# Graph network on one core: the message written feature-major, the degree spread by a bf16 product, the turning of the aggregate dropped

## The reference

```python
h = maximum(layernorm(x), 0)                          # 3125 nodes x 256
# first network, 50000 edges, src/dst lists
msg_input  = concat([h[src], h[dst], edge_features])
hid        = relu(msg_input @ mW1 + mb1)              # 512 wide
messages   = hid @ mW2 + mb2                          # 256 wide
aggregated = segment_sum(messages, src)
u          = relu(concat([h, aggregated]) @ uW1 + ub1)
x          = x + h + u @ uW2 + ub2
h = maximum(layernorm(x), 0)
# second network: three layers of segment_sum(norm * (h @ W)[src], dst) + b, gelu between them
x = x + layers(h)
```

## Time and profile before

| | us |
|---|---|
| median of 3 runs | 2052.21 |
| lowest, highest | 2049.65, 2060.61 |
| the profiled execution | 2049.62 |
| its span, first to last instruction | 2047.8 |
| mean granted TensorE clock | 0.925 of full speed |
| fused stage within it | 1217.5 to 1528.5 |

### The profile page before, as it was taken

The page is one execution under the profiler, slowest core; times in us unless marked ns, Lnnn a source line. Parts: engine busy times, 40 slices in busy tenths (PEclk is TensorE's granted clock), DMA queues, the critical chain, the costliest instruction groups (busy, mean ns, idle before and its releaser), DMA issues. The chain is left out here.

```text
span 2047.8 us, 34486 instructions
## 1 busy us (share of the span) xinstructions
PE 1817.7 (89%) x8786; PEld 1237.3 (60%) x8786; DVE 1542.7 (75%) x4650; ACT 797.9 (39%) x1975; POOL 1262.3 (62%) x1463
## 2 busy tenths in 40 slices
PE   4577887777399999999999998989979999999999
PEld 2344544444255555555555556666657888788887
DVE  7887787777489999999999988988988345445333
ACT  0122222222155665665665656656664112113000
POOL 2777777777788888888888859999979000000000
PEclk7677777888699999999999999999999999999999
DMA  5111111111276766666766785222236344343333
GB/s 163 39 58 51 52 58 58 58 58 56 69 197 195 198 195 195 198 195 195 196 196 194 194 173 163 69 66 68 72 92 185 93 124 124 93 126 121 109 108 110
DMA packets 181705, 254.12 MB, mean 124 GB/s; under 512 B 29244, under 2 KB 144761, under 8 KB 181514
## 3 DMA queue, kind: packets, MB, share of 16 engines
q0 software_dynamic: 47888, 126.25, 22.6%
q1 hardware_dynamic: 104696, 102.31, 16.4%
q10 hardware_dynamic: 28930, 23.35, 3.5%
HBM read 202.35 MB, written 49.37 MB: 123 GB/s over the span
## 5 line engine op out<-in xcount | busy, mean ns | idle before, releaser
L1009 POOL DMA_INDIRECT brow<-B_rows,rows x440 | 467.8, 1063 | 114.9 <-issue 58.4
L380 POOL DMA_INDIRECT src_list<-ring,ring_row x392 | 385.8, 984 | 156.7 <-issue 117.6
L1959 PE MATMUL pO<-F,y 128*128 128x512 f32 x1728 | 431.5, 404 | 4.7 <-DVE y L1770 3.2
L1959 PEld LDWEIGHTS pO<-F,y 128*128 128x128 f32 x1728 | 326.7, 190 | 79.8 <-DVE y L1770 4.0
L1332 POOL TENSOR_SCALAR src_oh<-iota,src_s 128x128 bf16<-128x128 bf16 x426 | 285.1, 685 | 39.9 <-PE pC L1475 21.8
L1059 PE MATMUL pNode<-hid_whole,oh 128*128 128x512 f32 x440 | 228.7, 601 | 4.9 <-DVE sums L1195 4.5
L1125 ACT ACTIVATE turned<-pC 128x256 fp32r<-128x256 bf16 x220 | 84.7, 385 | 279.9 <-PE pC L1038 279.9
L1348 DVE TENSOR_SCALAR dst_oh<-iota_cw,dst_s 128x458 bf16<-128x458 f16 x568 | 181.7, 366 | 0.0
L1061 PE MATMUL pNode<-hid_upper,oh 128*128 128x512 f32 x220 | 175.3, 797 | 0.0
L1475 PE MATMUL pC<-dst_oh,src_oh 128*128 128x458 bf16 x568 | 157.4, 361 | 16.6 <-SPq L1430 8.3
L824 PE MATMUL pP<-U,upto 128*128 128x182 bf16 x385 | 49.6, 280 | 136.4 <-DVE posf L587 136.4
(11 more groups left out here) (306 smaller groups left out, 3413.1 us busy)
## 6 DMA issues: line engine op xcount, KB each, us to landing
raw<-C_rows SPq DMA_DIRECT2D x54, 768.0 KB, 4.4
C_rows<-c_rows ACTq DMA_DIRECT2D x175, 114.5 KB, 1.7
raw_first<-C_rows SPq DMA_DIRECT2D x18, 768.0 KB, 4.4
rows<-src_list SPq DMA_DIRECT2D x110, 100.0 KB, 2.8
brow<-B_rows,rows POOLq DMA_INDIRECT x440, 3.8
U_parts<-part_u SPq DMA_DIRECT2D x25, 256.0 KB, 2.0
B_rows<-bst SPq DMA_DIRECT2D x25, 256.0 KB, 2.1
src_list<-ring,ring_row POOLq DMA_INDIRECT x392, 2.2
```

The costliest lines, as they stand in the source:

```text
L380: nc.gpsimd.indirect_dma_start(dr.src_list[:, :, :].rearrange("p t w -> (p t) w"), bass.IndirectOffsetOnAxis(ap=ring_row[:, k % RING, t:t ...
L1009: nc.gpsimd.indirect_dma_start(brow[:, t % BR, :], None, dr.B, bass.IndirectOffsetOnAxis(ap=rows_i[:, m % LCS, j, 1:2], axis=0)).then_inc( ...
L1959: last = mm(pO[m % 2][half][:, :], y[:, win, part, half * P:(half + 1) * P], F[:, n % FS, :], start=(win == 0 and part == 0), stop=False)
```

## The change

In `build_and_update` three things are different, and two types follow from them.

**Message with features on the partitions.** The operands of the message product are exchanged: `mw2` is now the stationary one and `sT` the moving one, so `pG` holds 128 features of the first half, then 128 of the second, by 128 nodes. That is the layout that the hidden product wants in `aggT`. The two transposes of PE (L1534), DVE's `agg` step (L1398) and DVE's copy (L1404) are gone.

**Degree spread over the partitions.** With features on the partitions, `mb2` is a column (one number for each partition, `[P, 2]`), and the degree is a row that every partition needs. A product with the column of `pair_w` repeated 128 times as the stationary operand gives that row on all partitions: four bf16 products in every second turn, for two windows, into the upper half of `pG`. `pair_w` and `degT` become bf16 for it. DVE copies the two rows to `degs` (in every second turn) and makes `aggT` with two instructions of 128 x 128.

**Order on DVE.** This work stands at u = 8 of the same turn, behind L1411 and L1413; it no longer waits at u = 4 and u = 7. SP loads `mb2` as two DMAs of one column each, in place of one that repeats the row over all partitions.

```diff
@@ DVE, build_and_update @@
                     if u == 1 and i == 0:
                         dve.wait_ge(gathered, 1)
-                        v.tensor_copy(keep.deg_src[:, :], pX[:, 0:NW]).then_inc(deg_read, 1)
+                        v.tensor_copy(keep.deg_src[:, :], pX[:, 0:NW]).then_inc(keep.own, 1)
+                        link.n += 1
@@
-                    if u == 4 and i < NW:
-                        dve.wait_ge(agg_done, i + 1)
-                        if i >= 1:
-                            dve.wait_ge(at_done, i)
-                        else:
-                            dve.wait_ge(deg_read, 1)
-                            dve.wait_ge(w_in, 16 * 5)
-                        v.scalar_tensor_tensor(out=agg[:, :], in0=mb2[:, :], scalar=keep.deg_src[:, i:i + 1],
-                                               in1=pG[:, 0:D], op0=ALU.mult, op1=ALU.add).then_inc(agg_ready, 1)
-                    if u == 7 and i < NW:
-                        dve.wait_ge(at_done, i + 1)
-                        if i >= 1:
-                            dve.wait_ge(u_done, i)
-                        v.tensor_copy(aggT[:, :], pG[:, D:2 * D]).then_inc(at_ready, 1)
@@ behind L1413 @@
+                    if u == 8 and i < NW:
+                        dve.wait_ge(agg_done, i + 1)
+                        if i >= 1:
+                            dve.wait_ge(u_done, i)
+                        else:
+                            dve.wait_ge(w_in, 16 * 6)
+                        if i % 2 == 0:
+                            some = min(2, NW - i)
+                            link(v.tensor_copy(degs[:, 0:some, :].rearrange("p n k -> p (n k)"), pG[:, D:D + some * P]))
+                        for q in range(2):
+                            v.scalar_tensor_tensor(out=aggT[:, q * P:(q + 1) * P], in0=degs[:, i % 2, :],
+                                                   scalar=mb2[:, q:q + 1], in1=pG[:, q * P:(q + 1) * P],
+                                                   op0=ALU.mult, op1=ALU.add).then_inc(at_ready, 1)
@@ SP @@
-            sp.dma_start(mb2[:, :], io["L0_gnn_mb2"].partition_broadcast(P)).then_inc(w_in, 16)
+            for q in range(2):
+                sp.dma_start(mb2[:, q:q + 1], io["L0_gnn_mb2"][q * P:(q + 1) * P].rearrange("(p o) -> p o", o=1)
+                             ).then_inc(w_in, 16)
@@ PE, message(i, half) @@
                     if i >= 1:
-                        pe.wait_ge(agg_ready, i)
-                        pe.wait_ge(at_ready, i)
+                        pe.wait_ge(at_ready, 2 * i)
                     else:
-                        pe.wait_ge(w_in, 16 * 5)
-                for k in range(2 * half, 2 * half + 2):
-                    last = mm(pG[:, 0:D], sT[:, k * P:(k + 1) * P], mw2[:, k, :], start=(k == 0), stop=(k == 3))
+                        pe.wait_ge(w_in, 16 * 6)
+                    if i % 2 == 0:
+                        for n in range(min(2, NW - i)):
+                            for m in range(KP):
+                                size = min(P, PAIRS - m * P)
+                                mm(pG[:, D + n * P:D + (n + 1) * P], pair_w[0:size, m, i + n:i + n + 1].to_broadcast([size, P]),
+                                   degT[0:size, m, :], start=(m == 0), stop=(m == KP - 1))
+                for k in range(4):
+                    last = mm(pG[:, half * P:(half + 1) * P], mw2[:, k, half * P:(half + 1) * P],
+                              sT[:, k * P:(k + 1) * P], start=(k == 0), stop=(k == 3))
@@ PE, turn loop @@
-                    if u == 7 and i < NW:
-                        pe.wait_ge(agg_ready, i + 1)
-                        for k in range(2):
-                            last = nc.tensor.transpose(pG[:, D + k * P:D + (k + 1) * P], agg[:, k * P:(k + 1) * P],
-                                                       keep.ident[:, :])
-                        last.then_inc(at_done, 1)
```

More of the change, by code:

```diff
@@ L1259, in build_and_update @@
         dst_oh = g.sb("dst_oh", [P, SLOTS, CW], BF16)
-        mb2 = g.sb("mb2", [P, D])
+        mb2 = g.sb("mb2", [P, 2])
+        degs = g.sb("degs", [P, 2, P])
         late_u = g.sb("late_u", [P, 8, 2, D])
         low, mw2, uw1, uw2 = keep.low, keep.mw2, keep.uw1, keep.uw2
-        agg, aggT = low[:, 16, D:2 * D], low[:, 17, D:2 * D]
+        aggT = low[:, 17, D:2 * D]
         sT, uT = keep.spans[:, 0:HID], keep.spans[:, HID:2 * HID]
@@ L1284, in build_and_update @@
         c_out = keep.c_out
-        deg_read = g.sem("deg_read")
         w_in, h_in = keep.w_in, keep.h_in
@@ L1289, in build_and_update @@
         agg_done = g.sem("agg_done")
-        agg_ready = g.sem("agg_ready")
-        at_done = g.sem("at_done")
         at_ready = g.sem("at_ready")
@@ L1492, in hidden @@
                 if m == 0:
-                    pe.wait_ge(at_ready, w + 1)
+                    pe.wait_ge(at_ready, 2 * w + 2)
                     if w >= 1:
@@ L2089, in build @@
                 keep.iota_cw = more.sb("iota_cw", [P, CW], F16)
-                keep.pair_w = more.sb("pair_w", [P, KP, NW])
+                keep.pair_w = more.sb("pair_w", [P, KP, NW], BF16)
                 keep.part_m = more.sb("part_m", [P, KT])
@@ L2101, in build @@
                                             else keep.spread[:, 8, D + q * P:D + (q + 1) * P])
-                keep.degT = keep.low[:, NW - 1, 0:KP * P].rearrange("p (m k) -> p m k", m=KP)
+                keep.degT = keep.low[:, NW - 1, 0:KP * P // 2].bitcast(BF16).rearrange("p (m k) -> p m k", m=KP)
                 keep.chosen = lambda m, n: keep.rounded[:, (4 * m + 2 * n) * HID:][:, 0:HS]
```

## The result

The changed kernel runs in 2045.17 us (median of 19 runs, 2039.33 to 2054.25) against 2053.81 (median of 19, 2048.87 to 2060.61) for the kernel before: ratio **0.9956, 95% interval 0.9943 to 0.997**, so about 9.0 us less. That is 0.44%: the interval is clear of 1, but the gain is smaller than the half per cent that the prediction asked for before it would say faster. The profiled execution took 2042.46 us (span 2039.7) against 2049.62 (2047.8).

The account below looks back on a forecast made before the run. The chain between DVE and PE was taken to bound the kernel, with POOL and ACT next. -10.6 (waits) + 1.5 (start) = -9.1 us gave 2040.5 from the profiled execution, 2043.1 as a median; range 2036 to 2053.

Parts of the forecast that it names:

- The chain and its cure: Hidden product through DVE to update product, 2.36 us; with the relu done after 1.27, PE's wait of 0.83 us a turn goes.
- Two thirds of 15.9: Three timed stretches of the fused stage: 15.9 us above POOL's and ACT's floors, of which 10.6 was taken as gain.
- POOL's 70.5: Middle stretch of 42 buckets: POOL's busy time, 70.5 us, taken as the floor for its 77.8 us.
- ACT's floor of 91.3: Early stretch of 56 buckets: ACT's own pace would need 91.3 us, taken as the floor for its 96.6 us.
- ACT as the next bound: Fused stage: ACT's own sequence takes 1.63 us a bucket, 10.56 us a turn, and becomes a bound after the change.
- POOL beside it: Fused stage: POOL's one-hots need 10.56 us a turn, so POOL becomes a bound together with ACT.
- POOL's pace: POOL's one-hots stay at 0.669 us each; 0.681 throughout beside a full DVE would cost 4 us of the gain.
- PE's work about 0: Message pieces, removed transposes and degree product on PE sum to about 0, from -0.1 to +0.1 us a turn.
- DVE's new instructions: Two 128-column instructions of 0.34 us each, copy 0.21 a turn; sum 0.91 against 0.89 removed, so no change.
- PE's waits behind the `aggT` block: After the relu DVE stays with aggT, so PE waits 0.1 to 0.5 us for the next dst_oh; such waits rise.
- the `aggT` block starves PE: Rival, chance 0.10: a block behind the relu lasting over 2.1 us starves PE; at 2.6 us +14, so 2066.
- The start: Start of the fused stage: issuing and landing two single-column DMAs of mb2 costs +1.5 us, from +0.7 to +4.4.

Follow-up runs that it names:

- e1: Kernel before, only DVE's copy to aggT (L1404) moved from unit 7 to unit 8 behind the relu; ratio to before 0.9912.
- e2: Kernel before, DVE's copy to aggT moved to unit 8 but ahead of the sum and the relu; ratio to before 0.9923.
- e5: Changed kernel, ACT loads the register with the next bucket's end while the present copy runs; ratio to before 0.9899.
- e11: Kernel before, copy to aggT moved to unit 8 behind the relu and ACT's register load made early; 2033.52 us, ratio to before 0.9909.
- e6: Kernel before, only ACT's register load for the next bucket made early; ratio to before 0.9979.
- e9: Changed kernel plus a tiny ACT copy (128 x 1) ahead of each bank copy; one run, 2061.89 us.
- e10: Kernel before plus a tiny ACT copy (128 x 1) ahead of each bank copy; one run, 2058.56 us.
- e4: Changed kernel plus two dummy f32 transposes a turn on PE at unit 7; ratio to before 0.9959.
- e3: Changed kernel, its aggT block put back to unit 7, ahead of the sum and the relu; ratio to before 1.0066.
- e7: Changed kernel, the two mb2 column DMAs issued at the end of the block before, ahead of the loads of U; ratio to before 0.9913.
- e8: Changed kernel with ACT's register load early and the mb2 column loads early; 2037.27 us, ratio to before 0.9909.

## Why the prediction was right, step by step

The forecast was 2043.1 us, from -10.6 + 1.5 = -9.1; measured were 2045.17 us, and -9.0 by the ratio, -8.6 by stage and medians. That the sums agree to half a microsecond is in part luck, since the two terms missed in opposite directions (-11.4 for -10.6, +2.8 for +1.5). Most of the 2.1 us between forecast and measured time is the base: the kernel before came out at 2053.81 us, not at 2052.2.

- **The chain and its cure: right; the price of the wait was misread.** Hidden to update product 1.24 us from 2.36; relu done 1.15 us after the sum's start, 1.19 after the hidden product (1.27 forecast). e1 shows that the order alone is the gain, and e2 that nearly all of it comes with the one-hots moved ahead of what waits. The 0.83 us a turn that I called PE's loss was 19.2/23 from the row of the weight load; PE's own row gives 12.9/23 = 0.56. That wait went as forecast (0.5 us left in all). DVE's remaining wait is 9.5/16 = 0.6 us in the turns that have one, 0.4 a turn over all, where I said 0.3. The turns took (1495.8 - 1232.5)/24 = 10.97 us (L1407 below), inside the 10.8 to 11.0 named.
- **Two thirds of 15.9: right in the sum, wrong in its parts.** Forecast -10.6, measured -11.4 in the three stretches. The middle one reached the floor (70.7 us for POOL's 70.5, 7.0 of 7.3); the early one got 2.2 of 5.3, the late one 2.2 of 3.3. Two thirds was a mean that held for none of them. Why the early one stays 3.2 us above ACT's floor of 91.3 is open: e5, with a faster ACT, got only 1.0 of it, and e11, with the same ACT and the old products, 2.7. The floors are soft by about 1 us as well: e1 and e11 took 69.7 and 69.3 us in the middle stretch, under POOL's 70.5, which came from 70.48/104 = 0.678 us a one-hot there; e11 made them in 69.29/105 = 0.660.
- **ACT as the next bound: right**, shown from both sides (e5 against e6, e9 against e10). In the three stretches of after 145 of 161 copies come 1.60 to 1.66 us apart, where it had been 123. **POOL beside it: half right.** It was close behind, and became the bound only when ACT was relieved (e11).
- **POOL's pace: right.** 0.660 us with a fuller DVE, not 0.681. The rule of the Trainium skill (page "SBUF — State Buffer", section "Who interferes with whom") has held as far as this row shows: POOL's one-hots got no slower while DVE's busy share rose from 90% to 95%.
- **PE's work about 0: right within what can be seen.** The message is now eight pieces in a row:

```profile
1303.93 1.06 PE L1492 MATMUL pG<-sums 128*128 128x128 f32 x8
```

  One alone lasts 0.275 us, so (1.06 - 0.275)/7 = 0.11 each, half of the 0.21 of a 256-column piece, as the row of the hidden product had said. The rule on load and product pairs from the Trainium skill (page "TensorE: Matmul & The Clock Gate", section "Back-to-back issue gap") would have added 0.22 us a turn; the trace has none of it. The degree product, for which I took 0.15 us a turn, costs less: its four bf16 pieces, each with a weight load of its own, start 0.058 us apart, so 0.23 every second turn, 0.12 a turn. Removing the transposes saved some 2.0 us by e4, and e1, which keeps them, is no slower. The new order alone needs none of this.
- **DVE's new instructions: right.** L1409 took 341 ns (0.34 forecast), L1407 411 to 425 for two windows.

```profile
L1409 DVE SCALAR_TENSOR_TENSOR sums<-degs,mb,pG x50: 326/341/349, 1232.9 to 1496.3; 128x128 f32<-128x128 f32 x50
...
L1407 DVE COPY degs<-pG x13: 278/411/425, 1232.5 to 1495.8; 128x256 f32<-128x256 f32 x12, 128x128 f32<-128x128 f32 x1
```

- **PE's waits behind the `aggT` block: right at the place, wrong in total.** In the corner above PE runs out at 1301.64 and waits 0.28 us, within the 0.1 to 0.5 forecast. But I had expected the sum of PE's waits for `dst_oh` to rise from 6.5 us; it fell to 3.2, most likely since the one-hots made in DVE's former idle time remove such waits elsewhere (e1, with one copy behind the relu, has 1.7). My walk also has a slip: its own terms for an even turn give 1.27 + 1.15 + 0.36 = 2.8 us to the next `dst_oh`, not 2.7; the corner shows 2.66 to PE's start. I had looked at the one place where the change could hurt and not at those where it helped. The rival *the `aggT` block starves PE* needed a block of over 2.1 us; it lasts 0.61 to 1.06.
- **The start: the term was too small.** +1.5 forecast; measured +0.6 to the first bank copy, +1.5 in the first seven buckets, +0.6 behind the last stretch: +2.8 before rounding, inside the bounds of 0.7 to 4.4. The issue did as thought, 0.98 us for two in place of 0.35; landing did not: 2.2 to 3.1 us, less than either value I had.

```profile
1217.68 0.98 SPq L1422 DMA_DIRECT2D mb<-in_L_gnn_mb_dram  x2
...
1220.47 1.22 PE L1475 MATMUL pC<-dst_oh,src_oh 128*128 128x458 bf16 x4 [1.57 <-SPq L1430]
...
1223.83 0.63 PE L1489 MATMUL pG<-sums,pair_w 128*128 128x128 bf16 x4
1224.26 2.02 PE L1492 MATMUL pG<-sums 128*128 128x128 f32 x8
```

  The first message starts at 1224.26, so the columns, landed by 1221.3 at the latest, did not hold it up. What I had not priced is the clock. In after, PE ran at 1.2 GHz (0.50) for 3 us longer:

```profile
1222.00:1225.00 3.00, 2.29 (x10) 1.63 (x11) 3.00 (x12) 1.08 (x2) 3.00 (x5) 0.50 0.43 138
1225.00:1228.00 3.00, 3.00 (x15) 2.66 (x14) 1.53 (x6) 0.00 (x0) 1.24 (x2) 0.50 0.53 164
1228.00:1231.00 3.00, 3.00 (x18) 2.09 (x18) 1.71 (x6) 1.66 (x4) 2.16 (x4) 0.97 0.45 127
```

  Before, the same windows had 0.53, 1.00 and 1.00. Over the traces this goes with the late columns, though not with them alone. All five kernels that load the columns at the start of the stage (after, e3, e4, e5, e9) are at 0.50 for 6.8 us and take 14.5 to 15.9 us for the first seven buckets. The two that load them earlier (e7, e8) are at 0.50 for 3.4 us and take 13.9. Of the seven with the old `mb2`, five have 3.4 us at 0.50, e10 has none and e1 has 6.8; they take 13.0 to 13.6 us, but e1 14.5. In e10 PE had waited for SP at the start about as in before (0.91 and 1.12 us, against 0.91 and 1.21), so these waits alone do not decide it. That the late columns bring the longer stretch at half clock is likely by this count and not shown; the cause is open.

## What to carry to other kernels

When two engines wait for each other, look first at the order in which the waiting engine issues what it has: independent work belongs ahead of the wait, and a single instruction that waits for the same event as a more urgent one behind that one. Here the first half was worth 11.8 us in the stretches (e2) and the second 0.8 more. Size the gain by what the *next* engines leave, stretch by stretch, and check it by making the next engine faster and slower: an edit worth 1 us of the stage before and 7 us after (e6, e5) is the clearest sign that a bound has moved. Read a wait from the row of the engine that does the work, not from that of its weight loads. When a rewrite brings a new order with it, try the order alone; here it was all of the gain, and with one register load moved on ACT more than twice that, -21.6 us against -8.6 in the stage (one trace each) and -0.91% against -0.44% by the ratios, of which the order alone has -0.88%.

## What the runs showed of the hardware

- A register load on ACT's queue, behind a copy, a refill and a store, cost about 0.5 us of each bucket in which ACT's compute side stood idle: copies 1.63 us apart with it, down to 1.08 when the load was issued while the copy was running (e5).
- A small ACT copy of 0.19 us lengthened a period by only 0.09 us (e9): the next copy started 0.09 us behind its start, before it had ended.
- DMAs of a single column (128 x 4 bytes) landed in 2.2 to 3.1 us at the start of this stage and took 0.36 to 0.57 us to issue, against 8.0 us and 0.51 to 0.89 for those in the earlier trace rows.
- TensorE's granted clock fell to 0.50 between 2 and 5 us into the stage in 13 of the 14 traces, and stayed there for 3.4 or for 6.8 us; the first seven buckets took 13.0 to 13.9 us with the 3.4 and 14.5 to 15.9 with the 6.8.
- The four bf16 pieces of 128 columns of the degree product, each with its own weight load, started 0.058 us apart; f32 pieces of 128 columns 0.11 us (after, clock 1.00).
